# How maxima, sums and state enter the attention products: wide products in place of many narrow ones

## The reference

```
# cross-attention, both layers (softmax subtracts each row's maximum)
scores = einsum('bqhd,bkhd->bhqk', q, k)          # layer 1: / sqrt(16)
attn = softmax(scores, axis=-1)
out = einsum('bhqk,bkhd->bqhd', attn, v)
# retention, layer 0, chunk by chunk
o_inter = einsum('bhid,bhde->bhie', qc * decay_q, S)
o = einsum('bhij,bhje->bhie', (qc @ kc) * D, vc) + o_inter
```

## Time and profile before

| | us |
|---|---|
| median of 3 runs | 2087.5 |
| lowest and highest | 2087.03, 2088.56 |
| profiled execution, first to last instruction (the page gives no other time for it) | 2244.8 |
| TensorE, products | 1840.0 busy, 19787 passes |
| TensorE, weight loads | 1448.8 busy |
| VectorE | 1169.0 busy |
| ScalarE | 625.2 busy |
| GpSimd | 873.8 busy |

### The profile page before, as it was taken

How to read it: one execution, slowest core, us unless ns; L and a number is a source line. 1 busy time by engine, 2 the same in 40 slices (tenths; PEclk the granted TensorE clock), 3 DMA queues, 4 the chain that set the end, 5 groups by cost and what they waited for, 6 DMA issues and landing times.

```text
span 2244.8 us, 49411 instructions
## 1 busy us (share of the span) xinstructions
PE 1840.0 (82%) x19787; PEld 1448.8 (65%) x19787; DVE 1169.0 (52%) x3042; ACT 625.2 (28%) x957; POOL 873.8 (39%) x977
## 2 busy tenths in 40 slices
PE   4898988988867599987787744889998659999994
PEld 2675655755654367765555533677776559999994
DVE  3465544544533024567655444677666534565654
ACT  0232212211212035554344511333333211111110
POOL 0003335336246800078888347563222310232223
PEclk9998877867768799998889876888888779999997
DMA  8304424424535947778787862221310141233232
GB/s 297 123 14 153 149 76 163 140 89 159 177 125 163 264 130 238 224 250 273 232 266 251 286 223 88 86 81 54 114 39 30 58 153 49 86 90 104 89 100 64
DMA packets 269648, 322.85 MB, mean 144 GB/s; under 512 B 25083, under 2 KB 245487, under 8 KB 268655
## 3 DMA queue, kind: packets, MB, share of 16 engines
q1 hardware_dynamic: 236399, 227.38, 31.9%
q0 software_dynamic: 33024, 92.32, 12.7%
HBM read 157.22 MB, written 162.40 MB: 142 GB/s over the span
## 4 chain that ended last, share of the span: by engine, by line
PE 64%; POOL 11%; issue 9%; DVE 6%; ACT 4%; DMA 4%; SPq 1%; another core or an unknown queue 1%; DVEq 0%; POOLq 0%; ACTq 0%
PE wide L2042 11%; POOL big L1416 7%; PE d_yp L2054 5%; PE bank L1186 5%; PE wide L1171 4%; PE wide L1174 4%; PE bank L1194 3%; PE wide L127 3%; PE wide L110 3%; PE bank L1006 3%; PE wide L1158 2%; POOL rest_ones L158 2%; ACT pt L657 2%; PE bank L1202 2%; PE bank L1065 2%
## 5 line engine op out<-in xcount | busy, mean ns | idle before, releaser
L1416 POOL DMA_INDIRECT big<-results,slots x256 | 264.1, 1032 | 247.9 <-DMA results<-e_y 170.5
L2042 PE MATMUL wide<-d_xt,d_ws 128*128 128x128 f32 x2272 | 278.4, 276 | 0.6 <-issue 0.6
L2042 PEld LDWEIGHTS wide<-d_xt,d_ws 128*128 128x128 f32 x2272 | 272.0, 193 | 4.5 <-issue 1.0
L595 POOL DMA_INDIRECT lists<-big,slots x160 | 155.1, 969 | 118.3 <-DMA lists<-big,slots 56.7
L657 ACT ACTIVATE pt<-wide 77x2048 f32<-77x2048 f32 x64 | 119.9, 1873 | 248.1 <-PE wide L1174 179.7
L849 DVE RECIPROCAL rden<-bank 128x256 f32<-128x256 f32 x64 | 112.3, 1755 | 144.7 <-PE bank L1186 91.8
L127 PE MATMUL wide<-shared_sw,shared_sh 128*128 128x256 f32 x512 | 125.0, 388 | 38.9 <-issue 24.0
L127 PEld LDWEIGHTS wide<-shared_sw,shared_sh 128*128 128x128 f32 x512 | 99.0, 194 | 81.4 <-issue 52.9
L1703 PE MATMUL wide<-e_xt,e_w1s 128*64 128x128 f32 x1280 | 97.4, 300 | 64.2 <-DVE e_w1s L1608 63.4
L1431 DVE SCALAR_TENSOR_TENSOR big<-big,weights 128x256 f32<-128x256 f32 x256 | 107.1, 480 | 82.5 <-DMA big<-results,slots 73.4
L551 POOL TENSOR_TENSOR rs<-mv,eps 128x4 f32<-128x4 f32 x32 | 6.5, 203 | 351.1 <-DVE mv L706 350.2
(11 more groups left out here) (277 smaller groups left out, 3779.0 us busy)
## 6 DMA issues: line engine op xcount, KB each, us to landing
lists<-zero SPq DMA_DIRECT2D x20, 2048.0 KB, 14.7
e_x<-lists SPq DMA_DIRECT2D x80, 512.0 KB
results<-e_y SPq DMA_DIRECT2D x80, 512.0 KB
d_x<-lists SPq DMA_DIRECT2D x71, 128.0 KB
results<-d_y SPq DMA_DIRECT2D x71, 128.0 KB
e_w<-in_L_w SPq DMA_DIRECT2D x2, 4096.0 KB
x<-in_x SPq DMA_DIRECT2D x8, 512.0 KB, 5.2
shared_sw<-in_x_t SPq DMA_DIRECT2D x32, 128.0 KB, 3.2
```

The costliest lines, as they stand in the source:

```text
L595: pool.indirect_dma_start(out=lists, out_offset=bass.IndirectOffsetOnAxis(ap=slots[:, b, i, k:k + 1], axis=0), in_=z2[i % 3][:, b, :], in_ ...
L1416: pool.indirect_dma_start(out=picked[:, c % NG, b, :], out_offset=None, in_=results[0:-(-PAGES_OF_STEP[s] // 4) * 4 * R0, :], in_offset=ba ...
L2042: ins = mm(out[T % 2][:, a * P:(a + 1) * P], ws[:, T % NW, n, c, a * P:(a + 1) * P], xt[:, T % 2, c], start=c == 0, stop=c == KC - 1)
```

## The change

Three edits, the first two in both layers.

Maxima: ScalarE's one move of the turned maxima into `peak_t` becomes four copies into `split`, copy n scaled by column n of `sel_at`, which is 1 on the partitions 32r+n and 0 elsewhere. In sc, four products of 512 columns, one for each strip r, take a matrix of ones as weights and the four masked copies as moving operand; they come first and start the banks. The 16 products of keys and queries then add to them. The 16 products with `sel` are gone, and so is `sel`; `all_ones` is set in its place. In layer 0 `split` lies in a free part of the large buffer.

Sums: in pv the 16 products with `ones` of 128 columns become 8 of 256, both halves c at once through a strided view of `pt`, and they come ahead of the products with the values.

State: in mix the 16 products of one head's state with the queries, in column strips, become four products of 128 columns whose weights are the states of four heads side by side. They are all issued first, and only the first of them starts the bank. The 16 products of values and `prob` follow as before.

```diff
--- before.py
+++ after.py
@@ -270,7 +270,7 @@
         head_mask = sb("head_mask", [P, P // XD])
         mask2 = sb("mask2", [P, 2])
         sel_at = sb("sel_at", [P, 4])
-        sel = sb("sel", [P, 4, CTX])
+        all_ones = sb("all_ones", [P, CTX])
         causal = sb("causal", [P, P])
         keys = sb("keys", [P, NB, KC, 2 * CTX])
         vals = sb("vals", [CTX, NB, XH, 2 * XD])
@@ -290,10 +290,10 @@
         mv = sb("mv", [P, 2, NB, 2])
         rs = sb("rs", [P, 2, 4, NB])
         if first:
-            peak, peak_t = units.sh[:, 0].rearrange("p (b n) -> p b n", b=NB), units.sh[:, 1]
+            peak = units.sh[:, 0].rearrange("p (b n) -> p b n", b=NB)
         else:
             peak = sb("peak", [P, NB, P])
-            peak_t = sb("peak_t", [P, TS])
+        split = spare[:, 4096:6144].rearrange("p (n t) -> p n t", n=4) if first else sb("split", [P, 4, TS])
         pt = sb("pt", [P, 2, XH * P])
         ctx_t = pt[:, 0, 0:NB * KC * CTX].rearrange("p (b c k) -> p b c k", b=NB, c=KC)
         att_t = sb("att_t", [P, KC, TS])
@@ -651,7 +651,10 @@
                 if stage == "q":
                     move(qt[:, p], filled(act, job)[:], job)
                 if stage == "mt":
-                    move(peak_t[:], filled(act, job)[:], job)
+                    ps = filled(act, job)
+                    for n in range(4):
+                        ins = nc.scalar.activation(split[:, n], ps[:], ACT.Copy, scale=sel_at[:, n:n + 1])
+                    empties(ins, job)
                 if stage == "sc":
                     ps = filled(act, job)
                     empties(nc.scalar.activation(pt[0:CTX, p % 2].rearrange("k (j n) -> k j n", j=4), ps[0:CTX],
@@ -720,7 +723,7 @@
             dve.wait_ge(consts, 16 * len(loads))
             make(nc.vector.tensor_reduce(mask2[:], head_mask[:].rearrange("p (m h) -> p h m", h=2), AX.X, ALU.add))
             make(nc.vector.tensor_reduce(sel_at[:], ident[:].rearrange("p (r n) -> p n r", r=4)[:, 0:4], AX.X, ALU.add))
-            make(nc.vector.tensor_copy(sel[:], sel_at[:].unsqueeze(2).broadcast_to([P, 4, CTX])))
+            make(nc.vector.memset(all_ones[:], 1.0))
             make(nc.vector.memset(ones_row[:], 1.0))
             make(nc.vector.memset(base[:], 0.0))
             make(nc.vector.memset(counts[:], 0.0))
@@ -1034,16 +1037,17 @@
                     emptied(pe, ("ret", i, p))
                     pe.wait_ge(state_done, i + 1)
                     for bb in range(2):
-                        b = 2 * p + bb
+                        for g in range(2):
+                            at = g * 2 * P + bb * P
+                            mm(out[:, at:at + P], state[:, 2 * p + bb, g].rearrange("p r n -> p (r n)"),
+                               qk[:, g, toks(2 * p + bb)], start=not (bb or g), stop=False, skip_group_check=True)
+                    for bb in range(2):
                         for g in range(2):
                             at = g * 2 * P + bb * P
                             for r in range(4):
-                                mm(out[quarter(r), at:at + P], state[:, b, g, r], qk[:, g, toks(b)], start=True,
-                                   stop=False, skip_group_check=True)
-                            for r in range(4):
                                 h = 4 * g + r
                                 of = (r * 4 + bb * 2 + g) * P
-                                ins = mm(out[quarter(r), at:at + P], v[:, b, h * RD:(h + 1) * RD],
+                                ins = mm(out[quarter(r), at:at + P], v[:, 2 * p + bb, h * RD:(h + 1) * RD],
                                          prob[:, p, of:of + P], start=False, stop=True, skip_group_check=True)
                     fills(ins, job)
                 if stage == "up" and first:
@@ -1165,26 +1169,27 @@
                     fills(ins, job)
                 if stage == "sc":
                     emptied(pe, ("mt", i, 0))
+                    for r in range(4):
+                        mm(out[0:CTX, r].rearrange("k (n t) -> k n t", n=4), all_ones[quarter(r)], split[quarter(r), :, toks(p)],
+                           start=True, stop=False, skip_group_check=True)
                     for n in range(4):
                         c, h = n // 2, n % 2
                         for r in range(4):
-                            mm(out[0:CTX, r, n * P:(n + 1) * P], keys[quarter(r), p, c, h * CTX:(h + 1) * CTX],
-                               qt[quarter(r), c, toks(p)], start=True, stop=False, skip_group_check=True)
-                        for r in range(4):
-                            ins = mm(out[0:CTX, r, n * P:(n + 1) * P], sel[quarter(r), n], peak_t[quarter(r), toks(p)],
-                                     start=False, stop=True, skip_group_check=True)
+                            ins = mm(out[0:CTX, r, n * P:(n + 1) * P], keys[quarter(r), p, c, h * CTX:(h + 1) * CTX],
+                                     qt[quarter(r), c, toks(p)], start=False, stop=n == 3, skip_group_check=True)
                     fills(ins, job)
                 if stage == "pv":
                     emptied(pe, ("sc", i, p))
-                    for what in range(2):
-                        for c in range(KC):
-                            at = (what * KC + c) * P
-                            for h in range(2):
-                                for r in range(4):
-                                    of = (r * 4 + c * 2 + h) * P
-                                    left = ones[:, h] if what else vals[:, p, c * 8 + 2 * r + h]
-                                    ins = mm(out[quarter(r), at:at + P], left, pt[0:CTX, p % 2, of:of + P], start=h == 0,
-                                             stop=h == 1, skip_group_check=True)
+                    four = pt[0:CTX, p % 2].rearrange("k (r c h n) -> k r c h n", r=4, c=KC, h=2)
+                    for h in range(2):
+                        for r in range(4):
+                            mm(out[quarter(r), KC * P:].rearrange("k (c n) -> k c n", c=KC), ones[:, h], four[:, r, :, h],
+                               start=h == 0, stop=h == 1, skip_group_check=True)
+                    for c in range(KC):
+                        for h in range(2):
+                            for r in range(4):
+                                ins = mm(out[quarter(r), c * P:(c + 1) * P], vals[:, p, c * 8 + 2 * r + h], four[:, r, c, h],
+                                         start=h == 0, stop=h == 1, skip_group_check=True)
                     fills(ins, job)
                 if stage == "wout":
                     emptied(pe, ("pv", i, 2 * p))
```

## The result

The change makes the kernel slower: 2103.41 us in the median of four runs against 2087.27 for the kernel before beside them, a ratio of 1.0086 with a 95% interval of 1.0064 to 1.0108. That is +18.0 us by the ratio and 16.1 by the two medians. The profiled execution of the kernel after spans 2097.9 us, that is its timed runs less a few microseconds. The profiled one of before had 2244.8, 157 more than its runs. These two traces can't be laid side by side yet, and the first experiment shows why: the kernel before, profiled once more, spans 2084.8. I call that run "again" and compare after with it.

A forecast was written before the change was run, and what follows sets the result against it. TensorE's own stream in the two attention phases was taken as the bound. Delay, clock and tile-shape terms of +21.7 us less 6.5 for pairs took 2087.5 to 2102.7 us, slower by 0.7%; whole range 2040 to 2114.

The forecast's parts named there:

- I read the stall mostly as the recording's own: Layer 0 steps beside GpSimd's scatters: about 147 us excess, blamed on profiling, a tenth taken as present in timed runs.
- Pairs: Fewer weight-load and matmul pairs in stalled layer 0 jobs: 65 us off the profile, 6.5 off timed runs, between 0 and 65.
- the stall is real: Rival: timed runs lose pairs at 109 ns in layer 0 too, so the change gives 2044 us; chance 0.30.
- Column time 0: Score products, pv sums and mix state products: new wide products take as long as the narrow ones, priced at 0.
- The rival's sum: Rival: the 512-column score products run one after another, 165 us more, 2265 us; chance 0.02.
- Four moves, layer 1, 8 x 1.6: ScalarE's four copies delay the first score job by 1.6 us in each of eight steps, nothing covering it: +12.8 us.
- Four moves, layer 0, 7 x 0.25 + 1.6: Copies mostly covered by v and kt work: +0.25 us in seven steps, +1.6 in the last, +3.3 in sum.
- Clock: Layer 1: added idle ahead of sc delays the return to the upper clock, 0.5 us a step, +4, range 0 to 13.6.
- Tile shape: Mix jobs: one more switch between full-array and column-strip products in 16 jobs, +1.6 us, range 0 to 3.2.
- Sum: Whole kernel: 12.8 + 3.3 + 4 + 1.6 = +21.7 us; less 6.5 for pairs, 2102.7 us timed.
- The span falls by tens of microseconds while the median rises.: Sign of a right forecast: profiled span falls from 2244.8 to about 2201 us while timed runs slow to 2102.7.
- The delay is swallowed: Rival: a partner that does not move holds TensorE later in layer 1, removing delay and clock terms: 2086 us; chance 0.10.

The follow-up runs named there:

- single-edit kernels of the quick kind: Kernel before with, singly, three more ScalarE copies ahead of its move, the state edit, or the sums edit: 2110.07, 2091.66, 2089.77 us.
- fill: Kernel after with 16 unused key products ahead of the wait for the copies in each layer 1 step: 2216.96 us, ratio to before 0.9889, long kind.
- moves: Kernel before with three more ScalarE copies of the same bank ahead of its one move into peak_t: 2110.07 us, ratio 1.0109, quick kind.
- moves1: Kernel before with three more ScalarE copies ahead of its one move, in layer 1 only: 2252.06 us, ratio 1.0055, long kind.

## Why the forecast came out

The number was 2102.7 and the runs gave 2103.4, on the quick kind. The mechanism of the slowdown in layer 1 holds: the delay alone makes a kernel as slow. The account of the stall, which decided the sign, was wrong in its reason, and that it left the right sign was luck: on the long kind the same change is faster (0.9918).

- *"I read the stall mostly as the recording's own."* This step failed. The earlier trace rows compared a profiled execution of the long kind with timed runs of the quick one: before takes 2088 us on one chip and 2232 to 2257 on four others. "Two executions that differ by 157 us differ by the profiler" does not follow; other conditions of the two could differ as well, and that would have given two forecasts, one for each kind. The sum that seemed to bear it out, 147 beside 157.3, was a coincidence in part. It set the steps with scatters against a step without, and the earlier trace rows has five of them, not six. Against the same five steps of again (59.8, 61.4, 61.0, 65.4 and 53.6) the excess is 110.6 us. Layer 1, for which the forecast counted nothing, has another 27.1, and the rest of the 160 us between the two spans, about 22, lies elsewhere.
- *Pairs, "-6.5", between 0 and 65.* Quick kind: 0, in quiet jobs by their length and in the steps with scatters because TensorE waits for GpSimd's chain there. Long kind: the change stands at -18 us where it is +18 on the quick one, so the relief is about 36 us (0.0168 +- 0.0037 of the time, 28 to 44). The size of 65 took 101 to 114 ns for each pair removed, and such a price doesn't hold (213 ns in one job). The rival "the stall is real" had the right sign for those chips, with 43 us gained where 18 were.
- *Column time 0.* Right: quiet sc 1.90 and pv 1.86 us; the pv edit alone 1.0003. The 512-column products run side by side: the eight passes take 1.10 us at 2.4 GHz with the pipeline's end, where one after another they would take 8 x 0.43 = 3.4, by the pass of the earlier trace rows. (The rival's sum is 2102.7 + 165 = 2268 us, not 2265.)
- *Four moves, layer 1, 8 x 1.6.* Right place and nearly the size: 8 x 1.82 = 14.6 us. The copies start 0.57 us apart and last 0.69, where the plain move's 0.54 and 0.60 stood in my term; the bounds of 1.3 to 2.2 held it.
- *Four moves, layer 0, 7 x 0.25 + 1.6.* The wait is 0.51 us longer in seven steps (2.88 against 2.37 from the last transpose) and 1.83 in the last, 5.4 us instead of 3.3. None of it shows in the phase: first to eighth step take 408.3 us in after and 414.5 in again. The single-edit kernels of the quick kind have 415.3, 420.8 and 418.6 there, so one execution tells 5 us in this phase from nothing only poorly. That the -6 are a gain is not shown. What the traces do show is the wait for ScalarE that shrinks by 1.1 us in a step with scatters (3.12 to 2.00) where TensorE is 0.51 us later at the scores and 2 x 0.21 slower in mix. A term was missing here: slack of TensorE in the five steps with scatters.
- *Clock, +4, 0 to 13.6.* Layer 1's 18.8 us in seven steps less 7 x 1.82 leave 6.1, 0.9 a step, where 0.5 was taken. The lower level holds 113 us of these steps instead of 77, and the first sc of a step is at 1.2 GHz for all but 0.1 us at most in six of seven; in again it is so in two of seven. The experiment fill shows the other side in one step; the exact share stays open.
- *Tile shape, +1.6, 0 to 3.2.* In quiet jobs the upper end: 16 x 0.21 = 3.4 us, a little above the bound. The edit alone, 1.0014 (0.9995 to 1.0032), allows it and doesn't prove it. The Trainium skill, "TensorEngine Tiling (Array Packing)", section Key Properties, says that a switch of mode drains the engine. The trace agrees with it in direction: the quiet mix job with one more switch takes 1.98 us instead of 1.77.
- *Sum.* Without any relief the steps gave +21.7, inside the measured 13.4 to 22.5. The tenth of the stall that I took off moved the number from 2109.2 to 2102.7, from 5.8 us off the median to 0.7, but no run shows such a tenth on the quick kind; it was luck. By the ratio's +18.0 the sums with and without it (15.2 and 21.7) are about equally good.
- *"The span falls by tens of microseconds while the median rises."* It fell by 147, and for the wrong reason: the two traces are of different kinds. "The delay is swallowed" fell with moves (+22.8) and moves1 (+12).

## What to carry to other kernels

Before taking a difference between a profiled execution and timed runs for the profiler's, ask whether they ran on the same chip and at the same time, and where that isn't known give a forecast for each case. Ask of each stage which engine sets its length: a gain or a delay of TensorE of about 1 us vanished in steps that GpSimd's scatters set. Where TensorE does set it, a wait on another engine's output costs its delay wherever nothing is queued ahead of it, however few instructions TensorE saves; put the work that doesn't need the data first and let the late operand close the sum. Fewer passes at equal column time bought nothing on the quick kind (1.92 to 1.90 us for a score job), and on the long kind about 36 us where their number times the stalled price gave 65.

## What was unexpected of the hardware

- The same kernel takes 2088 us on one chip and 2232 to 2257 on four others. On the long kind TensorE's stream breaks into four or five passes and 0.3 to 1.0 us of idle in steps where GpSimd scatters rows, with 124 to 135 instead of 162 to 186 GB/s moved in such steps of the kernel before. Its traces also hold a quarter fewer semaphore updates (18102 against 24818). What differs stays open: no chip was used at two times, no run is known to be without recording, and none took the scatters away.
- The price of a stalled pair isn't constant: 109 ns in one mix job of 64 pairs, 213 in one of 40.
- In the one pair of layer 1 steps compared, a score job of 40 pairs takes 3.63 us at 1.2 GHz behind an idle of 1.97 us, and 1.91 us with unused products in place of most of that idle.
